# Three groups of 8, 8 and 10 fields instead of two halves of 13 in a two-layer feature-interaction kernel

## The reference

```python
def _cin_layer(x_prev, x0, W, b):
    return jnp.einsum('bik,bjk,hij->bhk', x_prev, x0, W) + b[None, :, None]
e = jnp.stack([tbl_f[ids[:, f]] for f in range(26)], axis=1)   # [512, 26, 32]
x1 = _cin_layer(e, e, W1, b1)          # W1 [128, 26, 26]
x2 = _cin_layer(x1, e, W2, b2)         # W2 [128, 128, 26]
z = jnp.sum(jnp.concatenate([x1, x2], axis=1), axis=-1)        # [512, 256]
h = jnp.concatenate([z, dense_ctx], axis=1)
h = jnp.maximum(h @ W_top1 + b_top1, 0.0)
h = jnp.maximum(h @ W_top2 + b_top2, 0.0)
y = h @ W_top3
```

## Time and profile before

| | us |
|---|---|
| median of 3 runs (164.03 to 164.59) | 164.32 |
| the profiled execution, its own time | 164.4 |
| its span, first to last instruction | 162.7 |
| TensorE matmuls busy (weight loads) | 152.3 (143.7) |
| VectorE, ScalarE, GpSimd busy | 110.6, 84.4, 70.4 |
| first look-up on TensorE starts | 10.96 |
| first step matmul of tile 0, 1, 2, 3 starts | 30.73, 72.00, 102.65, 133.30 |
| mean granted TensorE clock | 0.989 |

### The profile page before, as it was taken

The page is one execution under the profiler, slowest core; times in us unless marked ns, Lnnn a source line. Parts: engine busy times, 40 slices in busy tenths (PEclk is TensorE's granted clock), DMA queues, the critical chain, the costliest instruction groups (busy, mean ns, idle before and its releaser), DMA issues.

```text
span 162.7 us, 3320 instructions
## 1 busy us (share of the span) xinstructions
PE 152.3 (94%) x1261; PEld 143.7 (88%) x1261; DVE 110.6 (68%) x342; ACT 84.4 (52%) x225; POOL 70.4 (43%) x76
## 2 busy tenths in 40 slices
PE   6989999699925999999999999999999999999994
PEld 6979899599914999998999999999999899999993
DVE  5829899999999495996667799455788952241000
ACT  1133479689660639654444676344448644560032
POOL 2777777726478272466455366437360000000000
PEclk9999999999996999999999999999999999999999
DMA  4998011055700022000010101001010000000000
GB/s 150 357 400 310 16 14 16 12 175 158 265 4 8 10 65 96 12 12 12 5 19 6 12 8 16 8 10 18 5 16 0 4 0 0 4 0 0 0 4 1
DMA packets 4930, 9.07 MB, mean 56 GB/s; under 512 B 1617, under 2 KB 3217, under 8 KB 4914
## 3 DMA queue, kind: packets, MB, share of 16 engines
q1 hardware_dynamic: 2130, 6.25, 11.0%
q0 software_dynamic: 2176, 1.12, 4.8%
q10 hardware_dynamic: 608, 1.49, 2.5%
HBM read 8.85 MB, written 0.00 MB: 54 GB/s over the span
## 4 chain that ended last, share of the span: by engine, by line
PE 61%; DVE 16%; POOL 10%; issue 4%; ACT 4%; DMA 4%; DVEq 0%; ACTq 0%
PE bank L367 13%; PE bank L380 13%; POOL rows L284 10%; DVE folded L741 9%; PE bank L375 8%; PE bank L314 8%; PE bank L419 5%; PE bank L389 4%; DVE prod L900 2%; ACT diag L557 2%; DMA idx<-in_ids_dram 2%; PE bank L409 2%; PE bank L407 2%; PE bank L412 2%; PE bank L396 2%
## 5 line engine op out<-in xcount | busy, mean ns | idle before, releaser
L284 POOL DMA_INDIRECT rows<-in_tbl_dram,idx x68 | 69.5, 1022 | 50.0 <-DMA rows<-in_tbl_dram,idx 30.6
L367 PE MATMUL bank<-diag,prod 128*128 128x108 f32 x256 | 31.4, 276 | 1.6 <-DVE prod L900 1.6
L367 PEld LDWEIGHTS bank<-diag,prod 128*128 128x128 f32 x256 | 30.3, 192 | 2.3 <-issue 2.0
L314 PE MATMUL bank<-small,idb 128*128 128x256 f32 (+1 forms) x72 | 22.6, 423 | 5.1 <-DVE w1p L680 4.6
L733 DVE COPY t<-bank 13x128 f32<-13x128 f32 (+2 forms) x48 | 12.6, 263 | 20.8 <-PE bank L375 20.3
L380 PEld LDWEIGHTS bank<-t,v 128*128 128x128 f32 x208 | 24.6, 192 | 1.4
L530 ACT COPY t<-bank 128x432 f32<-128x432 f32 x32 | 15.0, 522 | 19.4 <-PE bank L367 19.3
L380 PE MATMUL bank<-t,v 128*128 128x128 f32 x208 | 25.0, 276 | 0.0
L557 ACT ACTIVATE diag<-prod,quad 128x416 f32<-128x416 f32 (+2 forms) x44 | 20.9, 554 | 5.5 <-DVE prod L696 5.5
L680 DVE TENSOR_TENSOR w1p<-bank,chosen 128x320 f32<-128x320 f32 (+2 forms) x28 | 15.0, 536 | 9.1 <-PE bank L314 7.8
L375 PE MATMUL bank<-diag,prod 128*77 128x64 f32 x256 | 20.1, 230 | 0.0
(11 more groups left out here) (71 smaller groups left out, 172.6 us busy)
## 6 DMA issues: line engine op xcount, KB each, us to landing
idb<-in_idt_dram SPq DMA_DIRECT2D x4, 576.0 KB, 5.8
rows<-in_tbl_dram,idx POOLq DMA_INDIRECT x68, 2.4
wt<-in_W_top_dram SPq DMA_DIRECT2D x2, 512.0 KB
w2t<-in_w2t_dram SPq DMA_DIRECT2D x1, 768.0 KB, 12.0
small<-in_small_dram SPq DMA_DIRECT2D x1, 672.0 KB, 9.1
w1t<-in_w1t_dram SPq DMA_DIRECT2D x1, 640.0 KB, 4.1
small<-in_small_dram SPq DMA_DIRECT2D x1, 608.0 KB, 10.6
w1p<-in_w1p_dram ACTq DMA_DIRECT2D x1, 521.0 KB, 3.9
```

The lines of the kernel that those rows point to most:

```text
L284: pool.indirect_dma_start(rows[t][:, f, :], None, tables[f], bass.IndirectOffsetOnAxis(ap=idx[:, t, f:f + 1], axis=0)).then_inc(s_got[t][p ...
L314: mm = nc.tensor.matmul(ps[:, c], onehot[:, t % 2, e * P:(e + 1) * P], small[:, SPLACE[e]:SPLACE[e + 1]], start=True, stop=True)
L367: mm = nc.tensor.matmul(m0[:, g % GBANK, :, 0:JW], prod[:, G, 0:P], diag[:, G, :, :], start=True, stop=True)
```

## The change

The two halves become three groups: B (fields 0 to 7), C (8 to 15) and A (16 to 25). Pairs within a group (36 + 36 + 55) with the one make exactly the 128 columns of the first matmul, which still meets all fields. The 64 pairs of one field of B with one of C are in the second matmul and meet only the fields of A and the one: its stationary operand has 64 pairs and the 16 fields of B and C (80 columns), its moving operand 11 x 4 = 44 columns. There are 192 pair columns with the one.

- `z2_low` has 5 matmuls over all 128 rows instead of 8, `z1` 4 instead of 5.
- The products become `products_low` (eight instructions for the pairs within B and C, one for the 64) ahead of `s_pa`, and `products_last` (two instructions for each of eight quarters of the groups' range) behind it. Part 0 of a tile is now 16 fields, part 1 seven, part 2 three.
- Setup: folds of fields 0 to 15 onto 128 columns, four fields an entry; of 16 to 25 onto 192, two an entry; 16 cross rows of 224 columns (ctB), then 10 of 160 (ctA). The adds are 51 instructions of 5184 elements (`last_terms`, then `low_terms`). w1p has 640 columns instead of 521.
- Ten fields are looked up, 5 of 8 chunks and 5 of 10, in eight picks; 16 are gathered. `PACE`, `PAUSES`, `LOOKED`, `BEHIND` and the order of look-ups in the first z2 change with it. The look-ups of tile 0 follow folds 1 to 8.
- W2 comes in the parts 0 to 3, 4 to 15, 16 to 25.

```diff
-C1 = PAIRS - P
-C, D = (0, 5), (5, 6)
-JLOW = 11
+NB, NA = 8, 10
+A0 = 2 * NB
+SHIFTS = NA // 2
...
-PARTS = [(0, 13, COL_A, 5), (13, 23, COL_B, 17), (23, 26, COL_B + 10, 23)]
+PARTS = [(0, A0, COL_B, 7), (A0, 23, COL_A, 19), (23, FIELDS, COL_A + 23 - A0, 23)]
-PACE = [0, 0, 0, 0, 0, 1, 2, 3, 3, 4, 5, 6, 7, 8, 9, 10, 12, 13, 14, 15, 17, 18]
+PACE = [0, 0, 0, 0, 0, 1, 1, 2, 3, 4, 5, 6, 7, 8, 10, 11, 13, 14, 16, 17, 18, 19]
-SMALL = [0, 1, 2, 3, 4, 13, 14, 15, 16]
-CHUNKS = [8, 8, 8, 8, 10, 8, 10, 10, 10]
+SMALL = [0, 1, 2, 3, 4, 5, 6, 16, 17, 18]
+CHUNKS = [8, 8, 8, 8, 8, 10, 10, 10, 10, 10]
-PICKS = [(0, 2), (2, 4), (4, 5), (5, 6), (6, 7), (7, 8), (8, 9)]
+PICKS = [(0, 2), (2, 4), (4, 5), (5, 6), (6, 7), (7, 8), (8, 9), (9, 10)]
-LOOKED = [(0,), (1,), (2, 3), (4,)]
+LOOKED = [(0,), (1,), (2, 3), (4, 5)]
-W2PARTS = [(0, 6), (6, 14), (14, 26)]
+W2PARTS = [(0, 4), (4, 16), (16, 26)]
-SETUP = [("fold", j, 2) for j in range(0, FIELDS, 2)]
-SETUP += [("ctA", x, min(3, HALF - x)) for x in range(0, HALF, 3)]
-SETUP += [("ctB", x, min(3, HALF - x)) for x in range(0, HALF, 3)]
+SETUP = [("fold", j, 4) for j in range(0, A0, 4)] + [("fold", j, 2) for j in range(A0, FIELDS, 2)]
+SETUP += [("ctB", x, 2) for x in range(0, A0, 2)]
+SETUP += [("ctA", x, min(3, NA - x)) for x in range(0, NA, 3)]
-BEHIND = {2: 0, 3: 1, 4: 2, 5: 3, 6: 4, 7: 5, 8: 6}
+BEHIND = {1: 0, 2: 1, 3: 2, 4: 3, 5: 4, 6: 5, 7: 6, 8: 7}
...
-                    m1 = bank[b0 + 2][0:M1, :].rearrange("p (g r j) -> p g r j", g=GSTEP, r=QUADS)
-                    mm = nc.tensor.matmul(m1[:, g], prod[:, G, P:P + M1], diag[:, G, :, JLOW:], start=True, stop=True)
+                    m1 = bank[b0 + 2][0:M1, 0:NSTEP * J1].rearrange("p (g r j) -> p g r j", g=GSTEP, r=QUADS)
+                    mm = nc.tensor.matmul(m1[:, g], prod[:, G, P:P + M1], diag[:, G, :, A0:], start=True, stop=True)
...
+            pe.wait_ge(s_sf, HIGH)
+            z2(0, NA)
+            look_up(1, 2)
             look_up(1, 3)
-            pe.wait_ge(s_sf, HIGH)
-            z2(0, 7)
-            look_up(1, 4)
-            look_up(1, 5)
-            z2(7, HALF)
-            look_up(1, 6)
-            pe.wait_ge(s_eg, STEPS)
             for q in range(DONE["v1"], len(SETUP)):
                 make(q)
             pe.wait_ge(s_sf, DONE["v1"])
             z2_low(0, False)
+            look_up(1, 4)
+            look_up(1, 5)
             pe.wait_ge(s_sf, len(SETUP))
-            z2(HALF, FIELDS, True)
+            z2(NA, 18)
+            look_up(1, 6)
+            z2(18, FIELDS, True)
+            look_up(1, 7)
+            pe.wait_ge(s_eg, STEPS)
...
+def products_low(eng, prod, factor):
+
+    for d in range(NB):
+        n = NB - d
+        eng.tensor_tensor(prod[:, :, PB[d]:PB[d + 1]].rearrange("p g (c i) -> p g c i", c=2),
+                          with_dims(factor[:, :, 0:], (A0, GROUPS), (NB, 2), (1, n)),
+                          with_dims(prod[:, 0, COL_B + d:], (PCOLS, GROUPS), (NB, 2), (1, n)), ALU.mult)
+    return eng.tensor_tensor(prod[:, :, PBC:PAIRS].rearrange("p g (b c) -> p g b c", c=NB),
+                             with_dims(factor[:, :, 0:], (A0, GROUPS), (1, NB), (0, NB)),
+                             with_dims(prod[:, 0, COL_B + NB:], (PCOLS, GROUPS), (0, NB), (1, NB)), ALU.mult)
```

The adds, in the terms of one destination and up to two sources each:

```diff
+    for d in range(NB):
+        n = NB - d
+        ab = X_AB - X_CB
+        terms.append((with_dims(fold_a[:, 0, PB[d]:], (n, 2), (PAIRS, NA), (1, n)),
+                      with_dims(ct_b[:, d, ab:], (side, 2), (NB, NA), (CROSS_B + 1, n)),
+                      with_dims(ct_b[:, 0, ab + d:], (side, 2), (NB, NA), (CROSS_B + 1, n)) if d else None))
+    terms.append((with_dims(fold_a[:, 0, PBC:], (PAIRS, NA), (NB, NB), (1, NB)),
+                  with_dims(ct_b[:, 0, X_AC - X_CB:], (NB, NA), (CROSS_B, NB), (1, NB)),
+                  with_dims(ct_b[:, NB, 0:], (NB, NA), (1, NB), (CROSS_B, NB))))
```

More of the change, by code:

```diff
@@ L15 @@
 FIELDS = 26
-HALF = FIELDS // 2
-SHIFTS = HALF // 2 + 1
+NB, NA = 8, 10
+A0 = 2 * NB
+SHIFTS = NA // 2
 WRAP = SHIFTS - 1
-HPAIR = HALF * SHIFTS
-PAIRS = 2 * HPAIR + 1
-C1 = PAIRS - P
-C, D = (0, 5), (5, 6)
-JLOW = 11
[L26 to L44, removed]
+PB = [sum(2 * (NB - e) for e in range(d)) for d in range(NB + 1)]
+PA = PB[NB]
+PHALF = PA + SHIFTS * NA
+PONE = PHALF + NA // 2
+PBC = PONE + 1
+PAIRS = PBC + NB * NB
+assert PONE == P - 1 and A0 + NA == FIELDS
 ONE = FIELDS
 JW = FIELDS + 1
-J1 = JW - JLOW
+J1 = NA + 1
 H = 128
@@ L133, in sem @@
             return ctx.enter_context(nc.semaphore(name))
-        w1p = sb("w1p", [P, 2, PAIRS + 2 * CROSS])
+        w1p = sb("w1p", [P, 2, WCOLS])
         w1t = sb("w1t", [P, 2, 1 + GSLOTS, H])
@@ L146, in dlrm_tower @@
         b2x32 = sb("b2x32", [P, 1])
-        w1s = sb("w1s", [P, PAIRS + 2 * CROSS])
+        w1s = sb("w1s", [P, WCOLS])
         z1w = sb("z1w", [P, 1 + GSLOTS, H])
-        ct = [sb(f"ct{s}", [P, HALF, HALF, HALF]) for s in range(2)]
-        folded = sb("folded", [P, FIELDS, PAIRS])
+        ct_a = sb("ct_a", [P, NA, CROSS_A])
+        ct_b = sb("ct_b", [P, A0, CROSS_B])
+        fold_b = sb("fold_b", [P, A0, P])
+        fold_a = sb("fold_a", [P, NA, PAIRS])
         v0 = sb("v0", [P, FIELDS, H])
@@ L387, in z2_low @@
                 for x in range(GRAM):
-                    k = slice(0, C1 if x == GRAM - 1 else 64 + C1)
-                    mm = nc.tensor.matmul(Z2[:, 0:P], v1[k, x, :], t1[k, x, :], start=False, stop=end and x == GRAM - 1)
+                    mm = nc.tensor.matmul(Z2[:, 0:P], v1[:, x, :], t1[:, x, :], start=False, stop=end and x == GRAM - 1)
                 if end:
@@ L428, in layer3 @@
                 mm.then_inc(s_l3, 1)
-            for q in range(DONE["ctB"]):
+            for q in range(CROSSES):
                 make(q)
@@ L661, in _ @@
             linked()
[L662 removed]
+            for e0, e1 in ((0, SMALL.index(A0)), (SMALL.index(A0), len(SMALL))):
                 f0, n = SMALL[e0], e1 - e0
@@ L758, in _ @@
             one_hot(1)
+            dve.wait_ge(s_sf, DONE["ctB"])
+            terms = last_terms(fold_a, ct_b)
+            add(terms, 0, False)
+            add(terms, 1, True)
             dve.wait_ge(s_sf, DONE["ctA"])
-            low = low_terms(folded)
-            add(low, 0, False)
-            add(low, 1, True)
-            cross = cross_a(folded, ct[0])
-            add(cross, 0, False)
-            add(cross, 1, True)
-            dve.wait_ge(s_sf, DONE["ctB"])
-            cross = cross_b(folded, ct[1])
-            add(cross, 0, False)
-            add(cross, 1, True)
+            terms = low_terms(fold_b, ct_a, ct_b)
+            add(terms, 0, False)
+            add(terms, 1, True)
             for i in range(len(PICKS)):
@@ L789, in _ @@
                     turn(t + 1, 0)
-                    for i in range(5, len(PICKS)):
+                    for i in range(6, len(PICKS)):
                         pick(t + 1, i)
@@ new lines, in pair_columns @@
+def pair_columns():
+    cols = [None] * WCOLS
+    for d in range(NB):
+        for c in range(2):
+            for i in range(NB - d):
+                cols[PB[d] + c * (NB - d) + i] = (c * NB + i, c * NB + i + d)
+    for d in range(SHIFTS):
+        for i in range(NA):
+            cols[PA + d * NA + i] = (A0 + i, A0 + (i + d) % NA)
+    for i in range(NA // 2):
+        cols[PHALF + i] = (A0 + i, A0 + i + SHIFTS)
+    first, second, last = range(NB), range(NB, A0), range(A0, FIELDS)
+    blocks = [(PBC, first, second), (X_A, list(second) + list(first), last), (X_CB, second, first),
+              (X_AB, last, first), (X_AC, last, second), (X_BC, first, second)]
+    for at, outer, inner in blocks:
+        for k, (i, l) in enumerate((i, l) for i in outer for l in inner):
+            cols[at + k] = (i, l)
@@ L932, in layouts @@
     cols = pair_columns()
-    w1p = np.zeros((P, 2, PAIRS + 2 * CROSS), np.float32)
+    w1p = np.zeros((P, 2, WCOLS), np.float32)
     for c, pair in enumerate(cols):
```

268 lines of the change are left out of this document (112 added, 156 removed).

## The result

| us | before | after |
|---|---|---|
| median (lowest to highest, 4 runs each) | 164.25 (164.03 to 164.59) | 171.18 (169.75 to 172.46) |
| profiled execution; its span | 164.4; 162.7 | 171.28; 169.6 |
| first look-up | 10.96 | 12.96 |
| first step of tile 0, 1, 2, 3 | 30.73, 72.00, 102.65, 133.30 | 36.18, 78.05, 109.69, 141.35 |
| mean granted TensorE clock | 0.989 | 0.970 |

After to before: 1.0378, 95% interval 1.0312 to 1.0444; this ratio leaves out the execution of 172.46 us, which lies over 1.5% above the fastest and counts as slow. By the medians the change makes the kernel 6.9 us slower, where 4.2 were forecast, and the time is 0.4 us above the range; by the ratio it is 6.2 us slower, 170.5 us, just inside.

What follows compares the result with a forecast made beforehand. TensorE was taken as the bound (busy 94%), with VectorE setting the pace until 49.8 us. Terms 2.6 + 0.4 + 0.5 + 1.84 - 1.1 = 4.2 on 164.32 gave 168.5 us; 8-in-10 range 165.5 to 170.8.

Steps and rivals of the forecast that it cites:

- Term 1: Start: fold 1 waits for the 768 KB W2 part, landing at 12.7, delaying the first look-up to 13.6: +2.6 us.
- Rival 2: Start: the W2 part arrives in time, the start's delay shrinks to 0.3: 166.2 us, chance 0.13.
- Term 2: First pick to tile 1's first pick: dearer picks and products against cheaper adds and last-part products on VectorE: +0.4 us.
- Term 3: Tile 1's first pick to its first step: z1 stalls 2.3 us for z1w, step at 75.5: +0.5 us.
- Rival 1: TensorE's clock falls to half in the new idle time, mainly at the start: 170.2 us, chance 0.22.
- Term 4: Tiles 1 and 2: late third spread delays the relus, layer 2 stalls 1.5 us: +0.92 each, twice 1.84.
- Rival 3: Tiles 1 and 2: relus not late, -0.59 each instead of +0.92: 165.5 us, chance 0.07.
- Term 5: Tile 3, without look-ups or products: only TensorE's changed z2, z1 and step prices count: -1.1 us.
- Rival 4: Steps: moving columns set the second matmul's price, saving 1.06 + 0.16 us in each of three tiles: 164.8 us, chance 0.04.
- Rival 5: Products ahead of the last turn are not dearer (2.7 us), kernel faster than before: 160.5 us, chance 0.03.

Runs made afterwards that it cites:

- a_warm: The changed kernel with idle matmuls added in four of TensorE's waits (9, 10, 10 and 10), no other work changed: 167.13 us, ratio 1.0132 to the kernel before.
- b_warm: The kernel before with 17 idle matmuls added ahead of tile 1's third look-up: 162.82 us, ratio 0.9862 to the kernel before.
- a_turn: The changed kernel with the 64 cross-group products moved behind the turn of the last part: 167.53 us, ratio 1.0187 to the kernel before.
- a_wide: The changed kernel whose second matmul moves 64 columns again instead of 44, with the same 80 stationary columns: 170.13 us, one execution.

## Why the prediction was right or wrong

**Direction and places: right. Sizes: partly.** Slower, through the four places named. Each stretch below is measured from the timelines, in us more than the kernel without the change. The first difference holds all falls of the clock, the second only the one of before, the third none:

| stretch | forecast | after - before | a_warm - before | a_warm - b_warm |
|---|---|---|---|---|
| 1. to the first pick | +2.6 | +2.8 | +1.9 | +2.1 |
| 2. to tile 1's first pick | +0.4 | +0.4 | -0.3 | -0.5 |
| 3. to tile 1's first step | +0.5 | +2.9 | +0.5 | +2.0 |
| 4. tiles 1 and 2 | +1.84 | +2.0 | +2.0 | +2.0 |
| 5. tile 3 to the end | -1.1 | -1.2 | -1.2 | -1.2 |
| sum | +4.2 | +6.9 | +2.9 | +4.4 |

The forecast started from the rows of before, with its fall at 50.0, and had none in the new kernel: that is the second difference, and there it was 1.3 us too high, by terms 1 and 2. That the medians at full clock differ by 4.3 us (167.13 against 162.82), close to the sum of 4.2, is luck: term 3 is 1.5 us larger than forecast in that comparison, since before has lost its fall, and makes up for the other two.

**Term 1 (+2.6): the mechanism held, the size by luck.** The part landed at 11.86 (bounds 12.3 to 13.0, taken 12.7), the first look-up began at 12.96 (13.6 forecast), but at half clock, so that the first pick came at 15.01 against 12.20: +2.8. In a_warm it is 14.10, +1.9: the term without the clock is 0.7 less than forecast, by the landing. The 247 KB more cost 0.66 us (11.86 for 11.2), 374 KB/us, near the 413 GB/s that all transfers together reach from 9.0 to 11.9 in after. The 138 KB/us of the forecast is the mean of ScalarE's queue beside SP's; no run separates the two queues. The lower bound stands on no row shown: by the earlier trace rows w1p went at 521 KB in 3.9 us, 134 KB/us, no faster. Rival 2 (in time) is out.

**Term 2 (+0.4): its prices held, its sum with the help of the clock.** From first pick to tile 1's first pick 37.9 us for 37.5 before, but 37.2 in a_warm, where the look-ups ahead of the picks no longer run at half clock; adds 12.8 us for 13.0 to 13.2, products 5.17 for 5.2, last-part products (35.58 to 38.46) 2.88 for 2.9. Tile 1's picks started at 52.88 for 52.7. That the adds pay more across rows, some 1.9 ns an element, held for the new table: all at 1.04 would have taken 9.1 us. The Trainium skill (SBUF — State Buffer, Specifications (TRN2)) has a penalty for each access that crosses to a new 16-byte line, which agrees with it.

**Term 3 (+0.5): this is the step that failed.** It measured 78.05 - 52.88 = 25.2 us for 22.3 before, +2.9. The forecast had TensorE at look-up 2 by 53.4, from the time at which VectorE was ready, and did not follow TensorE's own chain from tile 0's first step. That step began at 36.18 behind 2.57 us of idle time and ran at half clock, so TensorE became the bound until 65.58 and the last look-up came at 64.86 (63.6 forecast). From layer 2's start to the step it was then 3.24 us instead of 1.89. In a_warm look-up 2 is back at VectorE's pace and the stretch takes 22.8 us, as forecast (75.5 - 52.7). How much of the 2.4 us too little is the late start and how much the half clock, no run separates. And the 22.3 us of before hold its own fall: b_warm needs 20.8 (49.70 to 70.54), so that the change costs 2.0 us here at full clock, not 0.5.

**Rival 1 (clock, 0.22) came true, three times instead of once.** The argument against it was that the idle times expected (3.3, 2.3, 2.9; measured 2.25, 2.48, 2.54) are shorter than the 4.2 us after which the earlier trace rows showed a fall. One row at 4.2 is no threshold: it shows that 4.2 was enough, not that 2.5 is too little. And the idle time ahead of tile 0's step was in no term at all, though before has 1.57 us at this place: the terms count what VectorE does up to there, not that TensorE's setup ends (33.6) sooner than the copies and products that the step needs. The price of one fall, 1.7 us, was of the right size: the three cost 4.05 together, 1.35 each, of 5.1 that three stretches of 3.4 us at half speed could lose.

**Term 4 (+0.92 each): held.** Steps start 31.64 and 31.66 us apart for 30.65, +1.0; the stall is 1.40 and 1.41 for 1.5. a_turn shows its cause. Rival 3 is out.

**Term 5 (-1.1): held.** Tile 3 from its step to the end of the last copy: 26.64 for 27.81, -1.17.

```profile
159.74 1.28 PE L397 MATMUL bank<-t,v 128*128 128x128 f32 x10
160.86 0.39 PE L402 MATMUL bank<-t,z1w 128*128 128x128 f32 x2
161.08 0.83 PE L404 MATMUL bank<-t,z1w 112*128 112x128 f32 x6
```

L397 and L402 take 1.12 + 0.22 = 1.34 (1.33 forecast); L384 is 69.4 ns for 70.6. Rival 4 is out by a_wide. The Trainium skill (TensorE: Matmul & The Clock Gate, LDWEIGHTS) agrees, since it counts stationary columns; what its section Back-to-back issue gap gives an isolated matmul by moving columns does not set the price here. Rival 5 is out by the 5.17 us.

**The range** ended 0.4 us below the median and 0.3 above the time by the ratio. It took in one fall of the clock with the upper bounds, not a second; that the result is so near its end is luck, since terms 1 and 2 without the clock are 1.4 us below the forecast.

## What to carry to other kernels

A new wait on TensorE costs its own length and possibly more: here falls of the clock followed most of the idle times of 2 us and more, and one such stretch cost about 1.4 us. So list TensorE's idle times of the changed kernel one by one, and price each as if the clock might fall. If more work stands ahead of a small transpose that a short chain hangs on (turn, spread, relu, layer 2), count it in every tile; here moving 2.2 us of products behind the turn brought back 4.2 at full clock. A kernel is compared fairly with another only at equal clock: here idle matmuls alone gave the old kernel all that the mended new one had won.
